# A wait for landing ahead of every eighth gather, in a fused graph layer on one core

## The reference

```
xn  = layernorm(x)
x   = x + segment_sum(edge_weight * xn[dst_col], row) @ W.T + b      # graph part
        + mix(xn)        # linear attention of 8 heads over 25 tiles of 128 nodes, then two 256x256 products, gelu
x   = x + ffn(layernorm(x))   # routed: 2 of 8 experts, 256 -> 512 -> 256, gelu
```

## Time and profile before

| | |
|---|---|
| median of 3 runs | 1011.53 us (1011.49 to 1013.69) |
| span of the profiled execution | 987.5 us |
| what lies around the span (median less span) | 24.0 us |
| PE, DVE, POOL, ACT busy | 803.2, 674.9, 585.1, 414.9 us |
| the changed loop's stretch | 318.9 to 795.3 us of the span |

### The profile page before, as it was taken

One profiled execution on the slowest core, in us unless ns is written; L12 is line 12 of the kernel. 1 busy time (PEld: TensorE's weight loads), 2 busy tenths in 40 slices (PEclk: granted clock), 3 DMA queues, 4 the chain that ended last, 5 costly groups with the idle time before them and its releaser, 6 DMA issues.

```text
span 987.5 us, 14025 instructions
## 1 busy us (share of the span) xinstructions
PE 803.2 (81%) x4353; PEld 652.3 (66%) x4353; DVE 674.9 (68%) x1936; ACT 414.9 (42%) x1008; POOL 585.1 (59%) x648
## 2 busy tenths in 40 slices
PE   7879848888887688878874887778787787999997
PEld 6659746777766365555653665556665555999997
DVE  8889728899775453544554567666786677866676
ACT  3638734676572043233322232222332226766552
POOL 3947676788877666766665556656666500333353
PEclk9989988999889798999997879878898899999999
DMA  7210132233324323333333233324333611000000
GB/s 234 86 49 1 33 90 67 83 92 87 87 84 110 93 80 91 110 94 101 90 108 86 74 92 90 108 75 117 91 112 87 83 35 54 12 17 28 22 29 30
DMA packets 38993, 76.87 MB, mean 78 GB/s; under 512 B 9811, under 2 KB 22536, under 8 KB 38920
## 3 DMA queue, kind: packets, MB, share of 16 engines
q0 software_dynamic: 21120, 57.70, 21.4%
q1 hardware_dynamic: 17800, 18.29, 5.8%
HBM read 69.48 MB, written 6.48 MB: 77 GB/s over the span
## 4 chain that ended last, share of the span: by engine, by line
PE 34%; DVE 18%; issue 11%; another core or an unknown queue 7%; ACT 4%; DVEq 1%; POOLq 0%; POOL 0%; ACTq 0%
PE bank L2000 13%; DVE X L1281 8%; PE bank L1791 7%; PE bank L1842 4%; DVE ARENA L1269 2%; PE bank L1749 2%; PE bank L1849 2%; PE bank L1628 1%; PE bank L1916 1%; PE bank L1919 1%; DVE ST L1021 1%; PE bank L1857 1%; DVE KS L1330 1%; ACT OIA L816 1%
## 5 line engine op out<-in xcount | busy, mean ns | idle before, releaser
L699 POOL DMA_INDIRECT ARENA<-xg_rows,ARENA x440 | 427.4, 971 | 219.2 <-issue 118.4
L1281 DVE TENSOR_TENSOR X<-bank,X 128x256 f32 x440 | 185.2, 421 | 229.2 <-PE bank L1791 106.6
L1791 PE MATMUL bank<-ARENA 128*128 128x256 f32 x880 | 247.2, 422 | 57.6 <-DVE X L1281 43.8
L1791 PEld LDWEIGHTS bank<-ARENA 128*128 128x128 f32 x880 | 174.2, 209 | 108.8 <-DVE X L1281 52.9
L1269 DVE TENSOR_SCALAR ARENA<-iota,ARENA 128x128 f32<-128x128 f32 x440 | 150.3, 347 | 0.0
L1749 PE MATMUL bank<-OIA,ASA 128*128 128x128 f32 x676 | 98.5, 315 | 16.7 <-DVE ASA L1199 5.8
L1749 PEld LDWEIGHTS bank<-OIA,ASA 128*128 128x128 f32 x676 | 97.0, 231 | 20.5 <-issue 19.4
L816 ACT ACTIVATE OIA<-iota,LANE 128x128 f32<-128x128 f32 x286 | 85.9, 389 | 13.9 <-PE bank L1749 13.6
L984 ACT ACTIVATE HF<-bank,FB 128x262 f32<-128x262 f32 (+1 forms) x96 | 46.8, 487 | 40.8 <-DVE HFL L1566 20.5
L860 ACT ACTIVATE NK<-bank 128x256 f32<-128x256 f32 x25 | 9.6, 383 | 118.5 <-PE bank L1842 105.2
L2000 PE MATMUL bank<-QH,W1L 128*128 128x262 f32 (+1 forms) x192 | 55.2, 288 | 2.3 <-DVE W1L L1527 1.7
(11 more groups left out here) (317 smaller groups left out, 1564.6 us busy)
## 6 DMA issues: line engine op xcount, KB each, us to landing
ARENA<-xg_rows,ARENA POOLq DMA_INDIRECT x440
FW1A<-in_exp_w SPq DMA_DIRECT2D x8, 512.0 KB
xg_rows<-XGS SPq DMA_DIRECT2D x12, 256.0 KB, 2.1
out<-YO SPq DMA_DIRECT2D x24, 128.0 KB, 1.7
X<-in_x SPq DMA_DIRECT2D x1, 1664.0 KB, 12.4
X<-in_x SPq DMA_DIRECT2D x1, 1536.0 KB, 8.1
FW<-in_exp_w SPq DMA_DIRECT2D x2, 512.0 KB, 5.1
QKVW<-in_qkv_wT SPq DMA_DIRECT2D x1, 768.0 KB
```

Of the source, the lines that this page charges most:

```text
L699: pool.indirect_dma_start(RING[:, at, :], None, xg_dram, bass.IndirectOffsetOnAxis(ap=SIX[:, c:c + 1], axis=0)).then_inc(gathered[at // HA ...
L1281: V.tensor_tensor(xt, pair_bank(pair)[:, half * C:(half + 1) * C], xt, ALU.add).then_inc(x_added, 1)
L1791: ins = T.matmul(pair_bank(pair)[:, u * C:(u + 1) * C], SEL[:, t % 2 * HAND + k, :], RING[:, h * HAND + k, :], start=True, stop=True)
```

## The change

Ahead of columns 132, 140, 148, ... 436 (39 of 308), GpSimd waits until the gather that it issued last (column c-1) has landed. `landed(c)` gives the semaphore of that column's hand and the count that it has then. No instruction is added or moved on any other engine.

```diff
+        BREATH = 8
...
+        def landed(c):
+
+            r, at = divmod(c, RC)
+            return gathered[at // HAND], 16 * (r * HAND + at % HAND + 1)
...
             pool.wait_ge(slots_ready, 2)
             for c in range(COLS_A, COLS):
+                if (c - COLS_A) % BREATH == 0:
+                    pool.wait_ge(*landed(c - 1))
                 gather(c)
```

## The result

The kernel before took 1011.51 us (median of 4 runs, 1007.99 to 1013.69), the changed kernel 974.35 us (4 runs, 972.20 to 976.95). The ratio is 0.9635, its 95% interval 0.9594 to 0.9677: 37 us faster. The prediction said 991.0 us, with a range of 981 to 1015. Its direction was right, its size was not, and the time lies outside the range.

A forecast was written before the change was run, and what follows sets the result against it. Bound: the chain of a step, from PE to ACT and DVE and back. Late reports healed gave 44 us, capped at 25.6 by GpSimd's own work, less 5: 20.5 us gained, 1011.5 - 20.5 = 991.0 us, range 981 to 1015.

The forecast's parts named there:

- those 24.0 us: Around the profiled span of 987.5 us: time outside it, taken to stay, giving 1011.5 us for the execution.
- 476.4 - 451 = 25.6 us: Loop of the 308 gathers: the most that can count of the 44 us, since GpSimd's own work takes 451 us.
- floor: GpSimd in the loop: its own work of 393.8 us, 451 us with the added waits; the loop can't be shorter.
- breath: GpSimd in the loop: one added wait for a landing, a pause of 1.81 us in place of 0.30, 1.5 us more.
- the 27.3 us: DVE's remote waits up to 530 us, the keys-and-queries part: 11 waits, all counted as gone.
- half of 34.9: DVE's remote waits after 530 us: about half the late reports began before 10 us, so 17 us counted as gained.
- rival A: Whole kernel: late reports have another cause, GpSimd stops because PE is late, nothing gained; 1011.5 us, chance 0.20.
- a long unbroken stream of gathers holds PE's reports back, and a pause frees them: Gather loop: late reports come from long gather runs; no run longer than 8 gathers, 9.7 us, gives together 44 us.
- B: Rival, gather loop: a pause too short to free much, only the first part gains; about 1001 us, chance 0.20.
- C: Rival, gather loop: GpSimd becomes the bound and nothing is healed; slower, 1015 to 1024 us, chance 0.14.
- D: Rival, the added waits: fulfilled at once, so no effect by itself; excluded, as the gather lands 1.5 us after its end.
- the ring's 85.1 us of pauses: GpSimd in the loop: real pauses with the ring full, waiting for a pair, set against 57 us of added waits.

The follow-up runs named there:

- breath4: The changed kernel with the wait ahead of every 4th gather instead of every 8th; 1045.47 us, ratio 1.030 to the kernel before.
- sixth_2: The changed kernel with waits only from column 266 on, every 6 gathers instead of 8; 989.5 us, ratio 0.973 to the kernel before.
- first_half: The changed kernel with the waits only up to column 265; ratio 1.0001 to the kernel before.
- base_again: The kernel before, unchanged, run and profiled once more; 1015.3 us, profiled span 1008.4 us.
- second_half: The changed kernel with the waits only from column 266 on; ratio 0.9597 to the kernel before.
- pause_op: The changed kernel with three small GpSimd memsets in a row in place of each wait; ratio 0.9766 to the kernel before.
- spread_op: The changed kernel with three memsets, one by one ahead of gathers 0, 3 and 6 of every eight, replacing the wait; 980.15 us, ratio 0.9657.
- old_landing: The changed kernel with each wait for a gather issued 7 to 12 columns earlier, so no pause; ratio 1.0057 to the kernel before.
- after_again: The changed kernel, unchanged, run again in a later batch; 974.68 us, ratio 0.9687 to the kernel before.
- lead14: The kernel before with gathers from column 132 on waiting for two more pairs, GpSimd at most 14 columns ahead instead of 18; ratio 0.9981.
- lead16: The kernel before with gathers from column 132 on waiting for one more pair, 16 columns ahead instead of 18; ratio 0.9989.
- phase4_2: second_half with the waits 4 columns later, still every eighth; 979.7 us, ratio 0.9638 to the kernel before.
- fine_op: The changed kernel with a small memset ahead of every gather from column 132 on, replacing the waits; 966.6 us, ratio 0.9686 to the kernel before.
- tenth_2: The changed kernel with waits only from column 266 on, every 10 gathers instead of 8; 991.0 us, ratio 0.978 to the kernel before.

## Why the prediction was wrong in its size

**The base of the sum failed first.** The step "the profiled execution's own time is its span and those 24.0 us" took the difference between two executions for something around the span. It is 1.75 us. The loop of an ordinary execution is 498 us, not 476, and a gain "of at most 476.4 - 451 = 25.6 us" was capped 22 us too early. With 498 in place of 476 the same sum, capped by the same floor, would have had room for all its 44 us and given about 1011.5 - 44 + 5 = 972 us. That it would have hit (974.35 measured) is luck in part, since the next two terms were wrong as well. The warning stood in my own numbers: 24 us for which no row existed.

**The floor was a little low.** A breath costs 1.75 us, not 1.5, so 39 of them make 68 us and the floor is 393.8 + 68 = 462, not 451. The loop measured 470.4 us, against the 450 to 460 that I had named (window of the gathers' line, with POOL's busy time and count, clock, DMA share and GB/s, beside the earlier trace rows):

```profile
318.00:788.40 470.40, 300.30 (x308) 0.91 0.35 96
```

That GpSimd becomes what is late next was right: the chain shows it, and breath4 and sixth_2 measure it.

**The place was wrong.** "In the keys-and-queries part I count the 27.3 us as gone", and half of 34.9 behind it. first_half gained nothing, though DVE's remote waits up to 530 us fell from 27.6 us in base_again to

```profile
DVE X L1289 <- remote: 11.8, 5, 7.7
```

there. So those waits had not been on the path. second_half gained everything, and through ACT's wait for HS and PE's behind it (first_half has 33.7 us of the latter, second_half 5.5). The earlier trace rows show HS with 6.78 us, and I had not summed it. A wait was counted because it was odd, not because it was on the path. The profile of before fits this: from 530 to 796 us PE waited 18.0 us for HS there, 38.5 us in base_again, and DVE's remote waits were much the same (30.0 and 35.8 us).

**The direction was right, and rival A fell.** The pace of the gathers is a cause, not a consequence: memsets that touch no datum of the loop are worth 23 to 35 us (ratios 0.977 to 0.966). That no wait for a landing is needed, pause_op and spread_op show; that such a wait without a pause does nothing, old_landing. The Trainium skill's "SBUF — State Buffer", in "Who interferes with whom", had stood for a gain of 0. The measurement decides against such a forecast: in this kernel a slower stream of gathers makes ACT's waits for PE's products about 2.7 us shorter each. It doesn't show contention in the memory: in the event of base_again PE's products start 0.22 us apart to the last, and what is late is the report behind them.

**The reading of the mechanism was half right.** "a long unbroken stream of gathers holds PE's reports back, and a pause frees them": by the semaphore records shorter runs do make late reports fewer and shorter (up to 6.3 us late without breaths, 4.3 with one every eighth gather, 1.9 at every sixth, none at every fourth). But the time doesn't follow from that alone: 0.47 us at every gather is as good as a breath, though the reports stay as late as before. And "remote" ahead of L1281 did not fall to ten waits: 20 are left. "In the keys-and-queries part all late reports began after 11 us" was misread: in the profile of before, the first report that is over 1 us late by those records belongs to work that ended 7 to 11 us behind the start of its run of gathers, in both parts (one at 1.5 us aside), so a run of 9.7 us has time for one. Of the 27.3 us counted as gone in the first part 9.3 were left, of the 34.9 us counted as half gone in the second 28.2.

**Rivals B, C and D.** B took its time from the quick execution too, and its picture, a gain in the first part only, is the reverse of what first_half and second_half show. C did not happen at 8: 68 us are less than the ring's 85.1 us of pauses. D was excluded rightly.

TensorE's granted clock doesn't carry the gain, as far as single profiles tell. From 530 to 796 us it was 0.83 in base_again and 0.90 in the changed kernel, but it was 0.83 too in pause_op and after_again, whose loops are as short:

```profile
530.00:796.00 266.00, 195.59 (x783) 151.51 (x784) 169.53 (x628) 69.45 (x115) 152.73 (x162) 0.83 0.31 87
```
```profile
530.00:796.00 266.00, 213.40 (x830) 161.45 (x829) 177.73 (x659) 76.70 (x127) 163.21 (x172) 0.83 0.36 95
```

(base_again and after_again; columns as in the prediction's windows, with the busy times and counts of PE, PEld, DVE, ACT, POOL, then clock, DMA share and GB/s.) In the same 266 us PE gets 830 instead of 783 matmuls done.

**What stays open.** Why PE's reports come late while gathers are issued every 1.25 us. Not the lead of GpSimd (lead14, lead16), not the semaphore tests (old_landing), not the place in the ring (phase4_2), not the lack of one long pause (spread_op, fine_op). tenth_2 has the mean spacing of fine_op and a longer stream at 1.25 us, and its loop is 13 to 20 us longer, in one profile; so besides the mean the evenness may count. A backlog that grows a little with every gather at full pace and drains in gaps would fit most rows of the table. The semaphore records hint at it: in fine_op four reports due at 534.13, 535.19, 536.05 and 536.95 come in that order at 538.82, 540.23, 541.65 and 547.38, the first three one gather (1.41 us) apart; where GpSimd stops, waiting reports come 0.06 us apart. What holds them is not recorded, nor was it tested whether they would be as late without the recording of a trace; and the step from there to the time of a whole kernel was not measured by itself, so I don't call it shown.

## What to carry to other kernels

Work out the difference between a profiled span and the time of the same execution before anything is summed; where it is larger than a few us, the profile is of another kind of execution, and caps taken from it are wrong. A producer that runs ahead of its consumer needs no more than the consumer's pace: if it streams at full speed and other engines' signals come late, try slowing it to just below the pace at which its data are used, and check that it doesn't become the bound. Before a wait's length is booked as a gain, look for the row in which the engine on the path waits for what it delays.

## What the runs showed of the hardware that was not expected

- ACT, DVE and GpSimd were let go together by PE, within 0.30 us, up to 6.35 us after the trace's end of PE's products, behind gathers issued every 1.25 us. The semaphore records show it for PE alone: 44 of its 114 reports from 530 to 796 us of base_again are over 0.5 us late, none of DVE's or ACT's; with a breath every fourth gather none of PE's is. At a mean spacing of 1.41 to 1.47 us ACT's waits fell from 6.0 to about 3 us each (4.4 in tenth_2).
- From the end of the last gather to the next one that waits for its landing, about 2.05 us passed as a rule, 6.2 us at most. A 128x400 memset on GpSimd took 0.43 to 0.45 us, a 128x96 one 0.20 us.
- One unchanged kernel took 997 us in one batch and 1013 to 1018 us in four others (medians), and a profiled execution of it had a span of 987.5 us in one case and 1008.4 us in the other. The changed kernel's medians were 974.35 and 974.68 us in two batches.
